# First attention with its front in a new order, and ScalarE's accumulator for the sums of exponentials in three attentions

## The reference

```python
# layer 0: grouped projections, heads of 64 (q, k) and 16 (v), relative positions
q = grouped_proj(query, Wq).reshape(b, s, N_HEAD, D_HEAD) * SCALE
k = grouped_proj(query, Wk, bk).reshape(b, s, N_HEAD, D_HEAD)
v = grouped_proj(query, Wv, bv).reshape(b, s, N_HEAD, D_MODEL // N_HEAD)
content_score = einsum('bind,bjnd->bnij', q + r_w_bias * SCALE, k)
pos_score = einsum('bind,tnd->bnit', q + r_r_bias * SCALE, r_head)
pos_score = rel_shift_gather(pos_score, s, shift=1)
attn_prob = softmax(content_score + pos_score, axis=-1)
attn_vec = einsum('bnij,bjnd->bind', attn_prob, v)
h1 = query + attn_vec @ Wo + bo      # then a layernorm with gamma, beta

# layer 1 (heads of 16) and layer 2 (heads of 64)
attn = softmax(einsum('bqhd,bkhd->bhqk', q, k) * scale, axis=-1)
out = einsum('bhqk,bkhd->bqhd', attn, v)     # then an output projection
```

## Time and profile before

| | us |
|---|---|
| median of three executions | 1903.97 |
| profiled execution, device time | 1889.7 |
| its span | 1888.0 |
| PE busy | 1543.2 (82%) |
| DVE busy | 753.8 (40%) |
| ACT busy | 652.8 (35%) |
| POOL busy | 379.3 (20%) |
| first attention (four groups) | 32 to 350 |
| second attention (layer 1) | 745 to 925 |
| third attention (layer 2) | 1225 to 1480, its feed-forward included |

### The profile page before, as it was taken

How to read it: one execution, slowest core, us unless ns; L and a number is a source line. 1 busy time by engine, 2 the same in 40 slices (tenths; PEclk the granted TensorE clock), 3 DMA queues, 4 the chain that set the end, 5 groups by cost and what they waited for, 6 DMA issues and landing times.

```text
span 1888.0 us, 30939 instructions
## 1 busy us (share of the span) xinstructions
PE 1543.2 (82%) x10048; PEld 1091.5 (58%) x10048; DVE 753.8 (40%) x2158; ACT 652.8 (35%) x1667; POOL 379.3 (20%) x449
## 2 busy tenths in 40 slices
PE   6887889568767877888897699499999998599993
PEld 4545556343222345555676588365666776588883
DVE  4536363651010266555534322344554324611112
ACT  2655656221000132666631011153544432113331
POOL 5202121110000023222200255221221100123331
PEclk9888686659676778999996599699999999559997
DMA  7413314428999510000004255200000200225543
GB/s 200 128 43 84 84 42 117 147 68 275 328 317 316 152 48 1 2 0 0 1 0 126 81 175 170 66 1 0 0 0 0 100 0 9 75 74 157 152 136 90
DMA packets 92810, 177.79 MB, mean 94 GB/s; under 512 B 35306, under 2 KB 53904, under 8 KB 90680
## 3 DMA queue, kind: packets, MB, share of 16 engines
q1 hardware_dynamic: 78528, 129.86, 23.6%
q10 hardware_dynamic: 7056, 30.67, 5.0%
q0 software_dynamic: 7136, 16.10, 2.8%
HBM read 149.61 MB, written 26.99 MB: 94 GB/s over the span
## 4 chain that ended last, share of the span: by engine, by line
PE 43%; issue 24%; DMA 12%; DVE 11%; ACT 4%; SPq 3%; POOL 2%; DVEq 0%; POOLq 0%; ACTq 0%
PE bank L1603 7%; DMA WM<-in_fc 7%; PE bank L2053 6%; PE bank L2041 5%; PE bank L2043 4%; PE bank L1795 3%; PE bank L1705 2%; DVE MXU L881 2%; DVE SMU L887 2%; PE bank L1787 2%; DMA pos_scratch<-SLOTS 2%; PE bank L1693 2%; PE bank L2009 1%; PE bank L1722 1%; DMA WM<-rows_out 1%
## 5 line engine op out<-in xcount | busy, mean ns | idle before, releaser
L1603 PE MATMUL bank<-XT,AREA 96*128 96x408 f32 (+1 forms) x640 | 239.4, 533 | 33.0 <-ACT XT L1379 15.7
L1603 PEld LDWEIGHTS bank<-XT,AREA 96*128 96x128 f32 (+1 forms) x640 | 122.1, 196 | 139.5 <-issue 100.3
L1693 PE MATMUL bank<-KZ,QT 128*102 128x102 f32 x1152 | 148.6, 272 | 7.0 <-ACT PB L1423 3.6
L1693 PEld LDWEIGHTS bank<-KZ,QT 128*102 128x102 f32 x1152 | 129.1, 184 | 23.6 <-issue 12.8
L628 POOL TENSOR_TENSOR RS<-VE,expo 102x4 f32<-102x4 f32 (+1 forms) x53 | 53.0, 1001 | 440.8 <-DVE VE L826 387.4
L642 POOL TENSOR_TENSOR PB<-PB,RCU 102x306 f32<-102x306 f32 x96 | 66.8, 696 | 346.7 <-DVE RCU L888 346.7
L2053 PE MATMUL bank<-WM,KZ 128*128 x660 | 121.1, 332 | 0.0
L2041 PE MATMUL bank<-KZ,SLOTS 128*128 128x128 f32 x660 | 116.0, 301 | 2.5 <-issue 2.5
L1705 PE MATMUL bank<-AREA,OT 128*102 128x192 f32 x384 | 92.6, 356 | 23.5 <-DVE SLOTS L1120 10.5
L2053 PEld LDWEIGHTS bank<-WM,KZ 128*128 128x128 f32 x660 | 108.7, 195 | 0.4
L2041 PEld LDWEIGHTS bank<-KZ,SLOTS 128*128 128x128 f32 x660 | 93.6, 199 | 16.5 <-issue 5.3
(11 more groups left out here) (308 smaller groups left out, 2724.4 us busy)
## 6 DMA issues: line engine op xcount, KB each, us to landing
AREA<-in_fc SPq DMA_DIRECT2D x10, 1536.0 KB, 19.3
SLOTS<-in_m3w SPq DMA_DIRECT2D x33, 384.0 KB, 3.3
WM<-in_fc ACTq DMA_DIRECT2D x5, 2304.0 KB, 18.0
WM<-in_fc SPq DMA_DIRECT2D x6, 1536.0 KB, 21.2
AREA<-in_fc ACTq DMA_DIRECT2D x4, 2304.0 KB, 20.5
SLOTS<-in_m1w SPq DMA_DIRECT2D x33, 256.0 KB, 2.6
AREA<-pos_scratch SPq DMA_DIRECT2D x16, 459.0 KB
pos_scratch<-AREA SPq DMA_DIRECT2D x8, 913.5 KB
```

Of the source, the lines that this page charges most:

```text
L1603: last = pe.matmul(dst, lhsT, rhs, start=n == 0, stop=n == len(pieces) - 1)
L1693: last = pe.matmul(psum[k][0:T, cols(j)], QT[:, tile, cols(bb)], KALL[:, unit % per_tile * (HEADS // per_tile) + tile, cols(bb)], start=Tr ...
```

## The change

Five edits that belong together, and one that stands alone.

- In the first attention TensorE's order becomes: query tiles 0 to 3, two pairs of element 0, query tiles 4 and 5, the other four pairs of element 0, the six pairs of element 1, the six key tiles, the values. All but the values turn in four banks (`FBANKS` = 2, 3, 6, 7). `moved(...)` waits stand before the pairs for the query tiles that they read.
- `VECTOR_TILES` = (1, 4): VectorE and no longer ScalarE empties these query and key tiles, with tensor_scalar operations (two a tile, as before on ScalarE).
- VectorE's turn becomes: queries, `finish_0` of the group before (the closing part of `attend_0`), preparation of the next group, keys, values, units. The last group is closed behind the loop.
- `POS_STEPS` becomes 0, 1, 2, 3, 4, 5.
- `passed` counts the fillings that the other engine empties. The signal that XN may be overwritten (`xn_taken`) is given by the first matmul of position scores and no longer by one of the values.
- In all three twelve-head attentions the exponentials get `accum_out=SMU[...]`, one column for each head, and VectorE's reduction of line 887 goes.

```diff
--- before.py
+++ after.py
@@ -66,7 +66,9 @@
 
 POS_PAIRS = ((0, 1), (3, 4), (2, 6), (5, 9), (7, 8), (10, 11))
 
-POS_STEPS = (0, 1, 2, 4, 5, 6)
+POS_STEPS = (0, 1, 2, 3, 4, 5)
+
+VECTOR_TILES = (1, 4)
 MARKS = tuple(range(8))
 
 W0_LOADS = 16 * (12 + 3 + 7)
@@ -803,6 +805,13 @@
                 give(ins, "power_in")
                 dve.wait_ge(sem["power_out"], at.take("power_out"))
 
+            def passed(banks, n=1):
+
+                for _ in range(n):
+                    k = at.bank(banks)
+                    at.one(f"bank_full{k}")
+                    at.one(f"bank_free{k}")
+
             def wide(ap, n):
 
                 return ap.unsqueeze(2).to_broadcast([ap.shape[0], ap.shape[1], n])
@@ -884,7 +893,6 @@
             def inverse_sums(n):
 
                 dve.wait_ge(sem["exp_ready"], at.take("exp_ready"))
-                step(dve.tensor_reduce(SMU[:, n % 4, 0:HPU], PB[n % 4][:, 0:HPU, :], AX.X, ALU.add))
                 give(dve.reciprocal(RCU[:, n % 4, 0:HPU], SMU[:, n % 4, 0:HPU]), "sums_ready")
                 dve.wait_ge(sem["sums_ready"], at.now("sums_ready"))
 
@@ -994,23 +1002,65 @@
             for w in (rw0, rr0):
                 give(ts(w, w, -0.125, None, ALU.mult), "scaled")
             def prepare_a0(g):
-                if isinstance(g, int):
+                if g == 0:
                     dve.wait_ge(sem["words_loaded"], 16 * GB)
                 else:
                     dve.wait_ge(sem["words_behind"], 16 * (NB - GB))
                 layernorm(h_of(g), xn, name="xn_ready")
                 step(tt(group(XA, g), XN[:], spread(bo0), ALU.add))
 
-            def attend_0(g):
-                values(V, 16, bv0)
-                attention(16, True, lambda bb, o, k: free(tt(a_of(g)(bb), o, a_of(g)(bb), ALU.add), k))
+            def queries(p):
+                if p not in VECTOR_TILES:
+                    return passed(FBANKS)
+                k = at.bank(FBANKS)
+                src = full(k)[:, 0:TG]
+                ts(QT[:, p, :], src, -0.125, rw0[:, p:p + 1], ALU.mult, ALU.add)
+                free(ts(QR[:, p, :], src, -0.125, rr0[:, p:p + 1], ALU.mult, ALU.add), k)
+
+            def keys(p):
+                if p not in VECTOR_TILES:
+                    return passed(FBANKS)
+                k = at.bank(FBANKS)
+                src = full(k)[:, 0:TG]
+                ts(KZ[0:64, 0, p, :], src[0:64], bk0[0:64, p:p + 1], None, ALU.add)
+                free(ts(KZ[64:128, 1, p, :], src[64:128], bk0[64:128, p:p + 1], None, ALU.add), k)
+
+            def finish_0(g):
                 layernorm(a_of(g), a_of(g), eps=1e-9)
                 step(tt(group(XA, g), group(XA, g), spread(gamma0), ALU.mult))
                 step(tt(group(XA, g), group(XA, g), spread(beta0), ALU.add))
                 step(tt(group(H, g), group(H, g), group(XA, g), ALU.add))
 
             prepare_a0(0)
-            in_turns(prepare_a0, attend_0, lambda: prepare_d(0, 0))
+            at.one("bank_free2")
+            at.one("bank_free3")
+            at.one("bank_free6")
+            at.one("bank_free7")
+            passed(XBANKS)
+            passed(TBANKS, 6)
+            for g in range(NG):
+                at.first_banks()
+                passed(XBANKS, 2)
+                for p in range(4):
+                    queries(p)
+                passed(FBANKS, 2)
+                for p in (4, 5):
+                    queries(p)
+                passed(FBANKS, 10)
+                if g:
+                    finish_0(g - 1)
+                if g + 1 < NG:
+                    prepare_a0(g + 1)
+                else:
+                    prepare_d(0, 0)
+                for p in range(6):
+                    keys(p)
+                values(V, 16, bv0)
+                attention(16, True, lambda bb, o, k: free(tt(a_of(g)(bb), o, a_of(g)(bb), ALU.add), k))
+                passed(TBANKS, UNITS)
+                passed(XBANKS, 12)
+            finish_0(NG - 1)
+            at.first_banks()
             mark("attn0_done")
 
 
@@ -1363,6 +1413,11 @@
             def free(ins, k):
                 give(ins, f"bank_free{k}")
 
+            def passed(k):
+
+                at.one(f"bank_full{k}")
+                at.one(f"bank_free{k}")
+
             def mark(name):
 
                 n = at.bank(MARKS)
@@ -1421,7 +1476,7 @@
                         for j in range(HPU):
                             p = PB[s % 4][:, j, :]
                             last = activation(p, p if pos else psum[k][0:T, cols(j)], ACT.Exp, scale=-1.0,
-                                              bias=MXU[:, s % 4, j:j + 1])
+                                              bias=MXU[:, s % 4, j:j + 1], accum_out=SMU[:, s % 4, j:j + 1])
                         give(last, "exp_ready")
                     if pos and s in POS_STEPS:
                         pos(2 + POS_STEPS.index(s) // 3, 2 * (POS_STEPS.index(s) % 3), 2)
@@ -1444,29 +1499,42 @@
                 free(activation(RT[:, p, :], full(k)[:, 0:NREL], ACT.Copy), k)
             with at.loop(act, NG) as g:
                 turned(XT)
-                for p in range(6):
-                    k = at.bank(XBANKS)
+                def queries(p):
+                    k = at.bank(FBANKS)
+                    if p in VECTOR_TILES:
+                        return passed(k)
                     src = full(k)[:, 0:TG]
                     activation(QT[:, p, :], src, ACT.Identity, scale=-0.125, bias=rw0[:, p:p + 1])
                     free(activation(QR[:, p, :], src, ACT.Identity, scale=-0.125, bias=rr0[:, p:p + 1]), k)
-                def pos_rows(bb, first=0, n=len(POS_PAIRS)):
+
+                def keys(p):
+                    k = at.bank(FBANKS)
+                    if p in VECTOR_TILES:
+                        return passed(k)
+                    src = full(k)[:, 0:TG]
+                    activation(KZ[0:64, 0, p, :], src[0:64], ACT.Identity, bias=bk0[0:64, p:p + 1])
+                    free(activation(KZ[64:128, 1, p, :], src[64:128], ACT.Identity, bias=bk0[64:128, p:p + 1]), k)
+
+                def pos_rows(bb, first=0, n=len(POS_PAIRS), banks=XBANKS):
 
                     if first == 0:
                         act.wait_ge(sem["pr_stored"], at.now("pr_ready") * 32 + 32)
                     for h0, h1 in POS_PAIRS[first:first + n]:
-                        k = at.bank(XBANKS)
+                        k = at.bank(banks)
                         src = full(k)[0:T, 0:2 * NREL].rearrange("p (h n) -> p h n", h=2)
                         free(activation(PR[bb % 2][:, h0:h1 + 1:h1 - h0, 0:NREL], src, ACT.Copy), k)
                     if first + n == len(POS_PAIRS):
                         mark("pr_ready")
 
-                pos_rows(0)
+                for p in range(4):
+                    queries(p)
+                pos_rows(0, 0, 2, FBANKS)
+                for p in (4, 5):
+                    queries(p)
+                pos_rows(0, 2, 4, FBANKS)
+                pos_rows(1, 0, 6, FBANKS)
                 for p in range(6):
-                    k = at.bank(XBANKS)
-                    src = full(k)[:, 0:TG]
-                    activation(KZ[0:64, 0, p, :], src[0:64], ACT.Identity, bias=bk0[0:64, p:p + 1])
-                    free(activation(KZ[64:128, 1, p, :], src[64:128], ACT.Identity, bias=bk0[64:128, p:p + 1]), k)
-                pos_rows(1)
+                    keys(p)
                 attention(pos_rows)
 
 
@@ -1768,6 +1836,33 @@
             pe.wait_ge(sem["halves_cleared"], at.take("halves_cleared", 2))
             with at.loop(pe, NG) as g:
                 xt()
+                def project(w, p6):
+
+                    k, p = claim(FBANKS)
+                    part, c = p6 // 3, (p6 % 3) * 128
+                    return filled(pe.matmul(p[:, 0:TG], w[:, part, c:c + 128], XT[:, part, :],
+                                            start=True, stop=True), k)
+
+                def pos(bb, first=0, n=len(POS_PAIRS), banks=XBANKS):
+                    for pair in POS_PAIRS[first:first + n]:
+                        k, p = claim(banks)
+                        for j, h in enumerate(pair):
+                            last = pe.matmul(p[0:T, j * NREL:(j + 1) * NREL], head(QR, h, 2, 64, cols(bb)),
+                                             head(RT, h, 2, 64, slice(0, NREL)), start=True, stop=True)
+                            if j == 0:
+                                say_taken(last)
+                        filled(last, k)
+
+                q_moved = [project(wq0, p6) for p6 in range(4)]
+                moved(*q_moved[0:2])
+                pos(0, 0, 2, FBANKS)
+                q_moved += [project(wq0, p6) for p6 in (4, 5)]
+                moved(*q_moved[2:4])
+                pos(0, 2, 2, FBANKS)
+                moved(*q_moved[4:6])
+                pos(0, 4, 2, FBANKS)
+                pos(1, 0, 6, FBANKS)
+                k_moved = [project(wk0, p6) for p6 in range(6)]
                 v_moved = []
                 for first in range(0, GB, 2):
```

(23 more changed lines are left out.)

## The result

The changed kernel has a median of 1840.39 us over four runs (1837.04 to 1842.37), the kernel before 1904.99 over four (1891.46 to 1914.15). The profiled executions are 1889.7 and 1837.04 us, 52.7 apart; the one of before is shorter than all four of its timed executions and the one of after the shortest of its four, and the medians are 64.6 apart.

The account below looks back on a forecast made before the run. ScalarE was taken to set the plain steps and, with two circulating banks, the first attention's front. Terms -21 - 16 - 1 + 9 + 2.4 = about -26 us gave 1863 or 1878, named 1870; own range 1852 to 1885, whole 1846 to 1930.

Parts of the forecast that it names:

- A step set by ScalarE goes from 1.23 to 1.53: Plain attentions: accumulator reads add 0.30 us to each ScalarE-set step; +9 us in the second attention, +2.4 in the third.
- The signs of being wrong: Plain steps of 1.8 us or more, a front over 33 us, or unit 12 waiting long for its load.
- The read's price: Each exponential's accumulator read costs ScalarE 0.10 us, with 0 and 0.28 as ends; 0.30 us a unit.
- The fronts: First attention, input copy to first exponential: earlier by 6.7, 1.3, 8 and 4.8 us in four groups, -21 in all.
- its last link: First attention's front: key tile 5 needs key tile 1's bank, which VectorE empties only after its closing and preparing work.
- The units of the first attention: The 15 unit steps of each first-attention group take 33.4 us against 37.7; -4 a group, -16 in all.
- TensorE stays at its high level: Rival: denser work keeps the first attention's groups at the higher clock; -12 more, -38 in all, 1852 us; chance 0.08.
- Steps 0 to 5: First attention's unit steps carrying position evacuations: 2.6 us four times and 2.9 twice, 16.2 us, about as now.
- The ends: End of each first-attention group, behind the last unit: -0.2 us each, -1 in all.
- the front gives nothing: Rival: low TensorE clock until tile 4 slips the first attention's front by 5 to 8 us; -5, 1885 us; chance 0.14.
- ScalarE pays more: Rival, all three attentions' units: read of 0.185 us gives 1906, 0.28 gives 1950; chances 0.17 (0.12 to 0.19), 0.25 (dearer).
- the case of a free read: All three attentions: accumulator reads cost ScalarE nothing; -56 us in all.

Follow-up runs that it names:

- the new front alone: Kernel before with only the new order of the front; VectorE still sums the exponentials; 1860.67 us.
- three small operations: Changed kernel with three more 1x1 ScalarE instructions behind the exponentials of each unit of the two plain attentions; ratio 0.976 to the kernel before.
- no sums after: Changed kernel without accumulators or any reduction, sums of the exponentials replaced by one; median 1835.8 us.
- late pairs: Changed kernel with the last three pair steps of the first attention's units one step later; 1841.02 us.
- plain sums: Changed kernel with accumulators in the second and third attention alone, VectorE summing as before in the first; 1849.95 us.
- the kernel with both sums: Kernel before with accumulators added to all 576 exponentials, written to an unread tile, VectorE's reduction kept; ratio 1.0079 to the kernel before.

## Why the prediction was wrong

**The failed step** is "A step set by ScalarE goes from 1.23 to 1.53". The plain step was not set by ScalarE. VectorE's three instructions filled it, TensorE's matmuls filled it as well (1.25), and ScalarE needed 1.01 of the 1.23 us. It went to 1.27, the steps with VectorE's copy of outputs fell from 1.83 to between 1.28 and 1.6, and two early ones from 1.54 and 1.31 to 1.02 and 0.98. So the second and third attention gave -5.4 and -6.6 (-3.6 without the slow group) in place of +9 and +2.4: 23 of the 26 us by which the profiles' difference exceeds the forecast. The evidence was misread: "ScalarE has no idle time ahead of those rows" was taken for saturation. The prediction itself noted that neighbours overlap by 0.09 us; then a row of 0.43 can end after a wait has begun and hide it. The idle time ahead of VectorE's rows and of TensorE's was not looked at in that stage. The signs of being wrong asked only for steps of 1.8 or more; steps below the forecast had no place among them.

**The read's price** was right: about 0.09 us each where 0.10 was taken, since exponentials come 0.32 apart in place of 0.23 (0.364 and 0.271 in the first attention). The row itself lasts 0.19 us and more; the rival that charged 0.185 is out. The advice of the Trainium skill, Perfetto Trace Analysis, section Optimizing Scalar/DVE Operations, to use fewer and larger operations on a saturated engine did not bear on this step, as the engine was not saturated. After the change it is, and the three small instructions of the experiment cost 0.28 us together.

**The fronts** were right: -21 forecast, -17.0 measured; 28.1 us for 27.8 in the third group, 31.0 for 31.1 in the fourth; the first gave 3.5 in place of 6.7, at a clock of 0.75. The chain was as described, and the kernel without its last link (all keys on ScalarE) confirms it. Two sizes in it erred in opposite ways, and the close hit is in part luck: VectorE's closing and preparing took 12.6 us and not 13.5, what follows it 8.0 and not 7.0. And the gain hangs on the low clock of the old order in two groups, which the prediction saw and did not call a matter of the profile. That the last link could be cut for about 20 us was not said.

**The units of the first attention** gave -20.9 for -16. The mechanism forecast, steps becoming shorter when VectorE's sum goes, is a quarter to a third of it: with the new front alone they already fall by 15.7. That part goes with the rival "TensorE stays at its high level", with a chance of 0.08: the clock of the four groups' units went from 0.82 to 0.84 up to 0.87 to 0.98 with the new front alone, and in the third group from 0.82 to 0.95 with the whole change. The sizes within were off too. Steps 0 to 5 were put at 2.6 and 2.9 us, though the terms named (0.9, 0.92, 0.30, later 0.40) make 2.1 and 2.5; in the third group these six took 14.6 us and not 16.2, and the nine behind 1.95 each and not 1.66.

```profile
205.29:237.35 32.06, 28.38 (x251) 21.06 (x247) 18.01 (x47) 26.27 (x116) 9.75 (x14) 0.95 0.34 93
```

The Trainium skill, TensorE: Matmul & The Clock Gate, section What's actually happening, says that activity releases the throttle; this row, with fewer holes and 0.95, agrees as far as one row can. That the transfers' holes closed and the clock rose for it is argued from the windows; no experiment set the clock alone. The ends gave -5.2 for -1, of which 4 is one end at the low clock in the first group of the kernel before (12.25 us at 0.50 against 8.29 at 0.94 in the next; the profile of the new front alone has one of 11.39 at 0.63).

**The rival "the front gives nothing"** is out; so is "ScalarE pays more". The range failed because no case had the bound elsewhere in the plain attentions. Its low end stopped short of the case of a free read, -56 us; the profiles' -52.7 is near that number, but the read is not free, so the nearness is luck.

**Open:** the stretch of slots and first MLP, untouched, takes 395.5 to 407.7 us over the fourteen profiles, and the start up to the first input copy, 8.1 us longer in the changed kernel, is long in five of them (38.8 to 40.4 us), all with the new front, and short in nine (32.3 to 34.9), five of these with the new front. The four experiments with a long start (three small operations, no sums after, late pairs, plain sums) ran on one chip, the eight with a short one on two others, so the chip is a suspect beside the kernel. Neither was tested. Both are as large as the terms that the prediction argued over.

## What to carry to other kernels

Absence of idle time ahead of an engine's rows is no saturation when its rows overlap. Take the step as start to start, compare it with the sum of start-to-start prices where nothing waits, and read all other engines' rows in the same stretch: those whose distances add up to the step are the ones that can set it. There can be two, as here, and then relieving one gives nothing: the regular step stayed at 1.25 us without VectorE's sum. A split that gives tiles to a "free" engine must be checked against what stands in that engine's queue: here two key tiles behind 12.6 us of closing work cost about 20 us. And where a stage has holes, the same work can have more than one length by TensorE's granted clock (here 30.9 us at 0.90 and 39.0 at 0.53), so a front's gain has to be read from several profiles.

## What the runs showed of the hardware

- The accumulator read of an exponential is an instruction of its own, 0.19 to 0.20 us in the first attention, 0.19 to 0.42 in the plain ones, and costs 0.09 us in a queue. A 1x1 instruction costs about the same (0.28 for three).
- Durations of ScalarE's rows are no guide in a queue: in two steps after the change, 2.5 us apart, equal exponentials last 0.36 (at 776.84, above) and 0.42 us while their starts stay 0.32 apart.

```profile
779.06 0.49 ACT L1472 ACTIVATE PT<-bank 102x306 f32<-102x306 f32 x1
779.37 0.42 ACT L1478 ACTIVATE ON<-bank,MXU 102x102 f32<-102x102 f32 x1
779.60 0.28 ACT L1478 ACTIVATION_READ_ACCUMULATOR ON<-bank,MXU 102x1 f32 x1
779.69 0.43 ACT L1478 ACTIVATE ON<-bank,MXU 102x102 f32<-102x102 f32 x1
```

- 0.3 us of extra work a unit on ScalarE, in the kernel with both sums, was followed by two TensorE steps at a granted clock of 0.52 or 0.53 in three groups of four, 1.9 us each time. The changed kernel with three small ScalarE operations a unit had no such steps.
